# LayerNorm output n made by ScalarE instead of VectorE in a two-layer cross-attention kernel

## The reference

```
# layer 0
q = x @ Wq + bq;  k = ctx @ Wk + bk;  v = ctx @ Wv + bv
w = softmax(q k^T / sqrt(512), axis = query rows)        # over t
y = w @ v + x
n = (y - mean(y)) * rsqrt(var(y) + 1e-6)                  # LayerNorm over 512
x1 = n * gamma + beta
# layer 1
Q = x1 @ Wq + bq;  K = ctx @ Wk + bk;  V = ctx @ Wv + bv
out = x1 + (softmax(Q K^T / sqrt(512), axis = keys) @ V) @ Wo + bo
```

## Time and profile before

| | us |
|---|---|
| median of 3 runs | 684.29 |
| the profiled execution | 682.88 |
| its span, first to last instruction | 680.8 |
| TensorE busy | 667.1 |
| VectorE busy | 520.4 |
| GpSimd busy | 490.3 |
| ScalarE busy | 424.6 |

### The profile page before, as it was taken

How to read it: one execution, slowest core, us unless ns; L and a number is a source line. 1 busy time by engine, 2 the same in 40 slices (tenths; PEclk the granted TensorE clock), 3 DMA queues, 4 the chain that set the end, 5 groups by cost and what they waited for, 6 DMA issues and landing times.

```text
span 680.8 us, 12411 instructions
## 1 busy us (share of the span) xinstructions
PE 667.1 (98%) x4047; PEld 589.4 (87%) x4047; DVE 520.4 (76%) x1227; ACT 424.6 (62%) x1037; POOL 490.3 (72%) x394
## 2 busy tenths in 40 slices
PE   8988999999999999999999999999999999999987
PEld 6975888989898898889889888988989898898976
DVE  4889687877868787786878778796877779687765
ACT  2765666576666747666575766656566665666542
POOL 0566968769596877959687795968778695866762
PEclk9998999999999999999999999999999999999999
DMA  9902005050220505032050503104040401302003
GB/s 296 317 6 77 32 2 171 1 170 0 73 96 0 169 0 170 0 94 76 0 169 0 170 0 121 48 10 159 0 170 0 142 28 40 129 0 78 1 1 124
DMA packets 34657, 53.47 MB, mean 79 GB/s; under 512 B 4560, under 2 KB 12752, under 8 KB 34640
## 3 DMA queue, kind: packets, MB, share of 16 engines
q1 hardware_dynamic: 34640, 53.26, 23.7%
HBM read 36.44 MB, written 16.81 MB: 78 GB/s over the span
## 4 chain that ended last, share of the span: by engine, by line
PE 89%; DVE 5%; POOL 2%; ACT 1%; DMA 1%; issue 1%; SPq 0%; DVEq 0%; POOLq 0%
PE bank L418 77%; PE bank L425 12%; DVE n L898 1%; DMA bk_b<-in_L_xattn_bk_dram 1%; POOL n L1215 1%; DVE stats L1054 1%; POOL wq_sb L1221 1%; DVE x_even L1049 0%; DVE rb L981 0%; DVE xT_lo L874 0%; DVE n L1065 0%; POOL rstd L1227 0%; ACT bank L747 0%; ACT n L715 0%; SPq L322 0%
## 5 line engine op out<-in xcount | busy, mean ns | idle before, releaser
L1234 POOL TENSOR_TENSOR prod<-n,u_b 128x512 f32<-128x512 f32 x64 | 81.5, 1297 | 44.7 <-DVE n L1065 39.3
L872 DVE SCALAR_TENSOR_TENSOR y_lo<-bank,terms,y_hi 128x512 fp32r<-128x512 f32 x64 | 48.0, 749 | 62.8 <-ACT y_hi L665 62.8
L1273 POOL TENSOR_TENSOR r<-r,beta_b 128x512 f32<-128x512 f32 x60 | 76.0, 1298 | 0.0
L1266 POOL TENSOR_TENSOR r<-n,gamma_b 128x512 f32<-128x512 f32 x60 | 75.7, 1299 | 0.0
L665 ACT ACTIVATE y_hi<-bank,terms 128x512 fp32r<-128x512 f32 x64 | 43.9, 686 | 39.9 <-PE bank L418 39.9
L1227 POOL TENSOR_TENSOR rstd<-var_eps,minus_half 128x2 f32<-128x2 f32 x32 | 22.4, 699 | 63.5 <-DVE var_eps L1061 63.4
L667 ACT ACTIVATE pc_hi<-bank 128x512 fp32r<-128x512 f32 x32 | 19.2, 598 | 68.2 <-PE bank L418 68.2
L1038 DVE SCALAR_TENSOR_TENSOR r<-bank,rinv,r 128x512 f32<-128x512 f32 x60 | 44.8, 747 | 11.2 <-PE bank L418 11.2
L418 PE MATMUL bank<-wv_hi,wc_hi 128*128 128x512 f32 x128 | 51.6, 403 | 1.8 <-issue 1.8
L747 ACT ACTIVATE bank<-e,neg 128x256 f32<-128x256 f32 x64 | 29.9, 468 | 35.1 <-DVE neg L1000 35.1
L418 PE MATMUL bank<-xT_hi,wqk_hi 128*128 128x512 f32 x128 | 51.2, 400 | 0.0
(11 more groups left out here) (201 smaller groups left out, 2355.0 us busy)
## 6 DMA issues: line engine op xcount, KB each, us to landing
out_dram<-r SPq DMA_DIRECT2D x15, 1024.0 KB, 5.4
x_even<-in_x_dram SPq DMA_DIRECT2D x8, 1024.0 KB, 7.2
ctxn<-in_ctx_dram SPq DMA_DIRECT2D x16, 512.0 KB, 3.7
x_odd<-in_x_dram SPq DMA_DIRECT2D x8, 1024.0 KB, 7.0
rb<-r_rows SPq DMA_DIRECT2D x15, 256.0 KB, 3.8
wq_sb<-in_L_xattn_Wq_dram SPq DMA_DIRECT2D x4, 256.0 KB, 3.4
wk_sb<-in_L_xattn_Wk_dram SPq DMA_DIRECT2D x2, 512.0 KB, 6.8
wv_sb<-in_L_xattn_Wv_dram SPq DMA_DIRECT2D x2, 512.0 KB, 9.2
```

The costliest lines, as they stand in the source:

```text
L872: i = dve.scalar_tensor_tensor(dst, src, bias, high.bitcast(F32), ALU.add, ALU.subtract)
L1234: pool.tensor_tensor(prod[j % 2][:], N[:, j, :], u_b[1][:], ALU.mult).then_inc(prod_ready, 1)
L1266: pool.tensor_tensor(r[:, j, :], N[:, j, :], gamma_b[:], ALU.mult).then_inc(scaled_ready, 1)
L1273: pool.tensor_tensor(r[:, j, :], r[:, j, :], beta_b[:], ALU.add).then_inc(resid_ready, 1)
```

## The change

n of a block is made by ScalarE as Identity(scale * y + bias) with scale = rstd and bias = -mean * rstd. VectorE makes only that bias, called `shift`, for the two blocks of a half in one instruction over 128x2. On VectorE `shifts(0)` and `shifts(1)` stand where n(0), n(1) and n(2), n(3) stood. On ScalarE `normalise(it, b)` stands: in iteration 0 behind the bias rows (b = 0) and behind `row_terms` of blocks 0, 1 (b = 1); in iterations 1 to 14 behind the rounding of `pc` 0 (b = 0) and behind `row_terms` of blocks 0, 1 at the end (b = 1); in iteration 15 behind the roundings of `pc` 0 and of `pc` 1. The wait until the old n is no longer read moves from VectorE to ScalarE.

```diff
@@ finish_first (ScalarE, iteration 0)
                 for j in range(J):
                     bias_of_rows(it, j)
+                normalise(it, 0)
                 next_row_terms0(it)
                 copy_bank(it, "u1", 0, u_b[1][:])
                 bv_wo(it)
                 round_bank(it, "wvo", 0, WVO[0][:, 0, :])
                 row_terms(it, (0, 1), 0)
+                normalise(it, 1)
                 round_bank(it, "wvo", 1, WVO[0][:, 1, :])
@@ ScalarE
+            def normalise(it, b):
+
+                if b == 0 and it.back:
+                    wait_filled(act, it, "nT", KD - 1)
+                    act.wait_ge(scaled_ready, it.times(J, 0))
+                act.wait_ge(shift_ready, it.times(2, b + 1))
+                for j in range(b * RT, (b + 1) * RT):
+                    act.activation(N[:, j, :], XN[it.parity][:, j, :], ACT.Identity, scale=rstd[:, j:j + 1],
+                                   bias=shift[:, j:j + 1]).then_inc(n_ready, 1)
@@ iteration (ScalarE)
                     for b in range(2):
                         round_bank(it, "pc", b, halves(PC[0], b))
+                        if it.before_last or (it.front and b == 0):
+                            normalise(it, b)
                 if it.more and it.back:
                     next_row_terms0(it)
                 if it.front and it.back and not it.before_last:
                     row_terms(it, (0, 1), 0)
+                    normalise(it, 1)
@@ norm_and_output (VectorE)
-                def normalise(j):
-                    dve.wait_ge(rstd_ready, it.times(2, j // RT + 1))
-                    dve.tensor_scalar(N[:, j, :], xn[:, j, :], mv[:, j, 0:1], rstd[:, j:j + 1], ALU.subtract,
-                                      ALU.mult).then_inc(n_ready, 1)
+                def shifts(b):
+                    dve.wait_ge(rstd_ready, it.times(2, b + 1))
+                    q = slice(b * RT, (b + 1) * RT)
+                    if b == 0 and it.back:
+                        dve.wait_ge(n_ready, it.times(J, 0))
+                    dve.scalar_tensor_tensor(shift[:, q], mv[:, q, 0], -1.0, rstd[:, q], ALU.mult,
+                                             ALU.mult).then_inc(shift_ready, 1)
...
-                    if it.back:
-                        wait_filled(dve, it, "nT", KD - 1)
-                        dve.wait_ge(scaled_ready, it.times(J, 0))
-                    normalise(0)
-                    normalise(1)
+                    shifts(0)
                     add(3)
                     statistics(3)
...
                 if it.before_last:
-                    normalise(2)
-                    normalise(3)
+                    shifts(1)
...
                 if it.front and not it.before_last:
-                    normalise(2)
-                    normalise(3)
+                    shifts(1)
```

More of the change, by code:

```diff
@@ L242, in two_cross_attentions @@
         var_eps = sb("var_eps", [P, J])
-        rstd = sb("rstd", [P, J])
+        rstd, shift = sb("rstd", [P, J]), sb("shift", [P, J])
         waited = sb("waited", [P, 2])
@@ L271, in two_cross_attentions @@
         var_ready, rstd_ready, n_ready = sem("var_ready"), sem("rstd_ready"), sem("n_ready")
+        shift_ready = sem("shift_ready")
         prod_ready, r1_ready = sem("prod_ready"), sem("r1_ready")
```

## The result

The changed kernel is slower: 687.13 us median of 9 runs against 684.04 us of 9 runs of before, ratio 1.0056 (95% interval 1.0038 to 1.0074). The medians lie 3.1 us apart, and the ratio, which goes by all the runs, stands for 3.8 us (2.6 to 5.1).

A forecast was written before the change was run, and what follows sets the result against it. TensorE, busy 98% of the span, was taken to bound the kernel, with time won or lost only in head and drain. +3.8 - 0.3 = +3.5 us on 684.29 gave 687.8 us, range 686.2 to 690.2.

The forecast's parts named there:

- Head, +3.8: First pair's preparation: ScalarE stops for the shift, delaying the u1 copy and GpSimd's work; TensorE restarts 3.8 us later.
- The second shift waits for the GpSimd sum: Head: VectorE may be held by GpSimd's sum, making n(2), n(3) about 2.3 us later, hidden either way.
- Steady pairs, 0: Loop pairs: n on ScalarE delays roundings by up to 0.30 us, within the cover, so the cost is 0.
- 0.29 us of margin are left: Steady pairs: between VectorE's first cut and TensorE's x projection, 0.29 us remain of 0.59.
- Drain, -0.3: Last front half to last back half: the shorter shift lets TensorE start the n transposes 0.3 us earlier.
- Clock: Head: the low clock after TensorE's restart again lasts 3.1 us despite the longer pause, so nothing changes.
- a low clock clearly over 3 us after the restart: Head: a sign that the forecast is wrong, if the low clock lasts clearly over 3 us after TensorE's restart.
- Rival 1: Head: clock stays low longer after the longer pause; doubled, it costs 1.55 us, giving 689.4; chance 0.08, earlier end 0.06.

The follow-up runs named there:

- e4: The changed kernel plus one ScalarE activation (bv0_b copied onto itself) behind n(2), n(3) in iterations 1 to 14; 694.2 us, ratio to before 1.0169.
- e11: The changed kernel measured once more, unchanged, beside other kernels; ratio to before 1.0060.
- e1: The changed kernel, but in iteration 0 alone VectorE makes n as before; median 683.51 us, ratio to before 0.9990.
- e5: The changed kernel with normalise(0) of iteration 0 moved behind next_row_terms0 and the u1 copy on ScalarE; ratio to before 1.0017.
- e2: The changed kernel with n made by Copy with a scale only, no bias, the mean not taken out; ratio to before 1.0038.
- e8: The kernel before with, in iteration 0, GpSimd's bvwo sums ahead of the second rstd and VectorE's wvo_lo cuts and dots ahead of n(2), n(3); ratio 0.9991.
- e6: The kernel before with 12 extra matmuls, result overwritten, in TensorE's pause ahead of the bo1 product; ratio 1.0008.
- e7: The kernel before with GpSimd's two bvwo sums ahead of rstd of the second half in iteration 0; ratio 1.0017.
- e10: The kernel before with GpSimd's sums and VectorE's cuts and dots moved earlier in iteration 0, plus 9 matmuls in the head's pause, 7 in the drain's; 681.64 us, ratio 0.9965.
- e9: The kernel before with 7 extra matmuls, result overwritten, in TensorE's pause ahead of the last transposes of n; ratio 0.9981.

## Why the prediction was right

The forecast was 687.8 us, the measured median 687.13; by ratio it was 1.0051 forecast and 1.0056 measured.

- *Head, +3.8.* Shown. In the two traces of ScalarE's new order without a low clock in the V products (e4, e11) the restart is 3.70 us later; e1 and e5 show that ScalarE's order makes it. Inside, n for two blocks was put 0.2 us too short (e2, where it isn't, restarts 0.19 us sooner), the way from it to the u1 copy 0.15 too long (it took 2.78 us, not 2.93), and rstd and sums together 0.1 too long.
- *The second shift waits for the GpSimd sum.* Left open by the prediction, and so it was: 2.29 us. It was hidden, as argued: the xT rounding at 68.16 waited for TensorE. But it stands in VectorE's queue, whose slack there was down to 0.48 us.
The Trainium skill (SBUF — State Buffer, "Who interferes with whom") has this: a VectorE instruction with two SBUF inputs contends with a GpSimd instruction that reads SBUF. The shift (2.29 against 0.15) and the dots of e8 (2.31 against 0.67) agree.
- *Steady pairs, 0.* The step "0.29 us of margin are left" failed, by size, and twice. An n took 0.81, not 0.71, so the queue was free 0.2 us later. And the margin was reckoned from the end of the cut to the start of the projection, of which 0.15 us is the handover (e4): only 0.14 would have been left. Together they use it up, and each pair lost 0.02 to 0.03 us, in all 0.3 to 0.45. e2, with n as short as reckoned, loses nothing and has 0.31 - 0.15 = 0.16 left; e4 shows that the changed kernel has none.
- *Drain, -0.3.* The mechanism was right, the size 0: the same 0.2 us came in twice, once in each pair of n on this path. e2 shows 1.65 instead of 1.96.
- *Clock.* The prediction put its price at no more than before, and named a low clock clearly over 3 us after the restart as a sign of being wrong. It was 3.3 to 4.3 us in the four traces of this order (changed, e11, e2, e4) against 3.1, and restart to projection took 5.1 to 5.6 us against 5.0. Rival 1 was thus right in part, by 0.1 to 0.6 us and not by its 1.55.

The mis-sized terms add up to 0.6 to 1.3 us in the traces (0.3 in the drain, 0.3 to 0.45 in the loop, 0.1 to 0.6 of clock, less 0.1 in the head), and this goes against the forecast. The two traces of the changed kernel thus account for 4.2 and 5.0 us (the 5.0 with the early low clock of the first), the forecast was 3.5, and the medians lie 3.1 apart. That the forecast came out so near the median owes something to chance; the head's 3.8, the largest term, doesn't.

## What to carry to other kernels

Where one engine is full in the loop, an edit that relieves another one is judged in the prologue and the drain: look in each in-order queue for what stands behind the instruction that gets the new wait, for it is paid in full even if it has nothing to do with the data. A cover of a few tenths of a us in a loop is soon gone when each added instruction takes a tenth more than reckoned, and what goes beyond it is paid once per pass. Take the handover off before calling a distance between two rows cover, and measure the loss by the period, not by idle time in the rows. When two chains are of equal length, relieving one alone shows no gain (e6, e7) until the other goes too (e10).

## What was not expected of the hardware

- An activation of 128x512 from SBUF with a scale and a bias read per partition took 0.808 us, with a scale alone 0.716.
- The granted clock after a pause of TensorE is not the same from execution to execution: the head's low time was 3.4 us in four traces (before, e7, e8, e9) and 6.8 in five (changed, e2, e4, e5, e11), and there was none in e1, whose pause was 1.56 us. After the 2 us pause in the drain the clock fell in 3 of 11 traces without a fill there (e1, e5, e8), at 1.6 to 1.7 us each.
- A VectorE instruction over 128x2, 0.15 us by itself, took 2.29 us beside a GpSimd one over 128x1024, and ended with it.
